# Query, key and value projections as products of float32r parts, and an earlier split of the second head's maxima

## Time and profile before

| what | value |
|---|---|
| median of 3 runs | 775.11 us (773.37 to 775.14) |
| profiled execution | 772.37 us, of which the span of instructions is 770.6 us |
| busy in the span | PE 707.3 us (92%), DVE 586.9 (76%), ACT 487.0 (63%), POOL 132.5 (17%) |
| granted TensorE clock | 0.995 of full, over the span |

### The profile page before, as it was taken

One profiled execution on the slowest core, in us unless ns is written; L12 is line 12 of the kernel. 1 busy time (PEld: TensorE's weight loads), 2 busy tenths in 40 slices (PEclk: granted clock), 3 DMA queues, 4 the chain that ended last, 5 costly groups with the idle time before them and its releaser, 6 DMA issues.

```text
span 770.6 us, 14200 instructions
## 1 busy us (share of the span) xinstructions
PE 707.3 (92%) x3976; PEld 373.9 (49%) x3977; DVE 586.9 (76%) x800; ACT 487.0 (63%) x886; POOL 132.5 (17%) x282
## 2 busy tenths in 40 slices
PE   5999999799889888998998888799999999998997
PEld 2456544522222222221222212388888888887886
DVE  5375588799999889899999984378777777756764
ACT  2472600388888888888888878656656665646321
POOL 1000000756531111011111111000000000005730
PEclk9999999999999999999999999999999999999999
DMA  9729100177411111011110172041111111122420
GB/s 316 246 68 328 44 1 0 47 234 235 130 48 32 32 32 32 17 32 32 32 32 24 38 262 90 15 151 44 51 54 49 46 54 54 54 90 81 143 92 28
DMA packets 49951, 65.35 MB, mean 85 GB/s; under 512 B 8168, under 2 KB 42880, under 8 KB 49920
## 3 DMA queue, kind: packets, MB, share of 16 engines
q1 hardware_dynamic: 38848, 40.85, 16.7%
q10 hardware_dynamic: 8000, 15.73, 6.2%
q0 software_dynamic: 3072, 8.39, 3.5%
HBM read 40.15 MB, written 24.38 MB: 84 GB/s over the span
## 4 chain that ended last, share of the span: by engine, by line
PE 76%; ACT 10%; issue 5%; DVE 5%; POOL 1%; DMA 1%; ACTq 1%; SPq 0%; DVEq 0%; POOLq 0%
PE ps L1386 14%; PE ps L1357 14%; ACT att L729 9%; PE ps L1410 9%; PE ps L1456 9%; PE ps L1238 7%; PE ps L1488 6%; DVE smax L993 3%; PE ps L1230 3%; PE ps L1503 3%; PE ps L1447 2%; PE ps L1198 2%; PE ps L1263 2%; PE ps L1346 1%; POOL acc L557 1%
## 5 line engine op out<-in xcount | busy, mean ns | idle before, releaser
L993 DVE TENSOR_REDUCE smax<-ps 128x2 f32<-128x1024 f32 x256 | 302.5, 1221 | 36.3 <-PE ps L1263 33.2
L729 ACT ACTIVATE att<-ps 128x512 f32<-128x512 f32 x512 | 267.7, 602 | 54.6 <-PE ps L1410 51.8
L1410 PE MATMUL ps<-att 51*128 51x512 bf16 x512 | 165.8, 384 | 32.8 <-ACT att L729 19.3
L1263 PE MATMUL ps<-att 48*128 48x512 bf16 x512 | 163.5, 386 | 1.4 <-DVE smax L993 1.4
L1357 PE MATMUL ps<-att,v_head 128*32 128x512 f32 x1024 | 137.1, 608 | 1.7 <-ACT o_sb L688 0.6
L1410 PEld LDWEIGHTS ps<-att 51*128 51x128 bf16 x512 | 39.7, 93 | 201.6 <-ACT att L729 95.8
L1386 PE MATMUL ps<-att_r 128*128 128x512 f32 x456 | 117.5, 406 | 3.1 <-DVE att_r L1054 1.6
L1050 DVE TENSOR_TENSOR att_r<-big,att_r 128x1024 fp32r<-128x1024 f32 x76 | 89.8, 1222 | 23.9 <-ACT att_r L709 23.8
L1386 PEld LDWEIGHTS ps<-att_r 128*128 128x128 f32 x456 | 85.5, 188 | 21.4 <-DVE att_r L1054 2.1
L709 ACT ACTIVATE att_r<-big 128x1024 fp32r x74 | 74.3, 1051 | 19.0 <-issue 19.0
L1456 PE MATMUL ps<-big,xn 128*128 x312 | 73.7, 380 | 0.0
(11 more groups left out here) (164 smaller groups left out, 691.1 us busy)
## 6 DMA issues: line engine op xcount, KB each, us to landing
big<-w ACTq DMA_DIRECT2D x8, 1024.0 KB
q_stacks<-big SPq DMA_DIRECT2D x12, 512.0 KB
att<-q_stacks SPq DMA_DIRECT2D x64, 96.0 KB, 2.1
slot_x<-zeros SPq DMA_DIRECT2D x1, 4992.0 KB, 17.2
e_x<-slot_x SPq DMA_DIRECT2D x39, 128.0 KB, 2.0
slot_y<-xn SPq DMA_DIRECT2D x39, 128.0 KB, 1.7
big<-w ACTq DMA_DIRECT2D x8, 512.0 KB
att<-k_stacks SPq DMA_DIRECT2D x64, 48.0 KB, 2.0
```

Source lines behind the costliest of these rows:

```text
L729: act.activation(probs[:, t % 2, g, :], ps[:, RING[turn_of(u) % 3], :], ACT.Exp, scale=SCALE)\
L993: dve.reduce_max(smax[:, s % 2, :].rearrange("p (half v) -> p half v", half=2)[:, :, v], ps[:, bank:bank + 2, :], X_AXIS).then_inc(max_don ...
L1263: return pe.matmul(ps[:, bank + half, :], q_st[s][rows, g, P * st:P * (st + 1)], k_st[s][rows, :], start=True, stop=True)
L1410: pe.matmul(ps[:, RING[turn % 3], :], k_st[s][rows, P * t:P * (t + 1)], q_st[s][rows, g, :], start=True, stop=True).then_inc(scores_ready, 1)
```

## The change

The weights of the three projections are rounded to float32r on ScalarE (`pw_hi`), and VectorE subtracts for the rest (`pw_lo`). For each quarter ScalarE rounds the two transposed banks (`round_xT`, into `p_hi`) in front of the two copies to `xnT`, and VectorE subtracts for the rest (`rest_of_xT`, into `p_lo`), with two buffers that alternate by quarter. A unit becomes three products of two matmuls each: hi weights by hi tokens, lo weights by hi tokens, hi weights by lo tokens. ScalarE's square roots stand one quarter earlier in its list. On GpSimd `split_max(1, 1)` stands in front of the memory sums. TensorE's own wait for the four loads moves from the first unit to the router matmuls; ScalarE waits for them before it rounds the weights.

```diff
@@ gpsimd
             split_max(0, 0)
             stage_v(0, 0, 0, 0)
+            split_max(1, 1)
             pool.wait_ge(s_add, 2 * 4)
@@ def steps
-                    if not (first and s == 0):
+                    if not (first and s < 2):
                         split_max(i, s)
+                    if not (first and s == 0):
                         stage_v(i, b, h0 + s, s)
@@ scalar
+            def round_xT(n):
+                act.wait_ge(xT_in_psum, n + 1)
+                if n >= 4:
+                    act.wait_ge(qk_in_psum, UNITS[n // 2 - 2][1])
+                act.activation(p_hi[n // 2 % 2][:, n % 2, :], ps[:, n % 4, :], ACT.Copy).then_inc(p_hi_ready, 1)
+            sqrt_var(0)
+            act.wait_ge(proj_loaded, 64)
+            act.activation(pw_hi[:, :, 0:2 * P], wq_sb, ACT.Copy)
+            act.activation(pw_hi[:, :, 2 * P:3 * P], wkv_sb, ACT.Copy).then_inc(pw_hi_ready, 1)
             for n in range(4):
-                sqrt_var(n)
+                if n < 3:
+                    sqrt_var(n + 1)
+                round_xT(2 * n)
+                round_xT(2 * n + 1)
                 copy_xT(2 * n)
                 copy_xT(2 * n + 1)
@@ vector
+            def rest_of_xT(n):
+                for m in (2 * n, 2 * n + 1):
+                    dve.wait_ge(xT_copied, m + 1)
+                    dve.tensor_tensor(p_lo[n % 2][:, m % 2, :], xnT[:, m % 2, 512 * n:512 * (n + 1)],
+                                      p_hi[n % 2][:, m % 2, :], ALU.subtract).then_inc(p_lo_ready, 1)
@@ at the end of quarter n's list, behind the writes of xn
+                if n == 0:
+                    dve.wait_ge(pw_hi_ready, 1)
+                    dve.tensor_tensor(pw_lo[:, :, 0:2 * P], wq_sb, pw_hi[:, :, 0:2 * P], ALU.subtract)
+                    dve.tensor_tensor(pw_lo[:, :, 2 * P:3 * P], wkv_sb, pw_hi[:, :, 2 * P:3 * P], ALU.subtract)\
+                       .then_inc(pw_lo_ready, 1)
+                else:
+                    rest_of_xT(n - 1)
+            rest_of_xT(3)
@@ tensor, project_qk
-                pe.wait_ge(xT_copied, 2 * n + 2)
                 wait(pe, qk_copied, u - 3)
-                for k in range(KD):
-                    tokens = xnT[:, k, 512 * n:512 * (n + 1)]
...
+                column = 2 * P if part == 0 else P * (part - 1)
+                for count, (ws, w_sem, xs, x_sem) in enumerate((
+                        (pw_hi, pw_hi_ready, p_hi, p_hi_ready), (pw_lo, pw_lo_ready, p_hi, p_hi_ready),
+                        (pw_hi, pw_hi_ready, p_lo, p_lo_ready))):
+                    pe.wait_ge(w_sem, 1)
+                    pe.wait_ge(x_sem, 2 * n + 2)
+                    for k in range(KD):
+                        last = pe.matmul(ps[:, 4 + u % 4, :], ws[:, k, column:column + P], xs[n % 2][:, k, :],
+                                         start=count == 0 and k == 0, stop=count == 2 and k == KD - 1)
                 last.then_inc(qk_in_psum, 1)
             for n in range(4):
                 transpose_xn(n)
-                if n == 0:
-                    pe.wait_ge(proj_loaded, 64)
                 for u in range(*UNITS[n]):
                     project_qk(u)
+            pe.wait_ge(proj_loaded, 64)
+            pe.wait_ge(xT_copied, 8)
```

More of the change, by code:

```diff
@@ L156, in build @@
         wkv_sb = big[:, 22016:22272].rearrange("p (k n) -> p k n", k=KD)
+        p_hi, p_lo = [[split[:, 4096 + 2048 * a + 1024 * n:5120 + 2048 * a + 1024 * n]
+                       .rearrange("p (k n) -> p k n", k=KD) for a in range(2)] for n in range(2)]
+        pw_hi, pw_lo = [split[:, 8192 + 768 * n:8960 + 768 * n].rearrange("p (k n) -> p k n", k=KD) for n in range(2)]
         mtmp = big[:, 4096:6144].rearrange("p (a d) -> p a d", a=8)
@@ L222, in build @@
         xT_copied = sem("xT_copied")
+        pw_hi_ready = sem("pw_hi_ready")
+        pw_lo_ready = sem("pw_lo_ready")
+        p_hi_ready = sem("p_hi_ready")
+        p_lo_ready = sem("p_lo_ready")
         lT_in_psum = sem("lT_in_psum")
@@ L569, in steps @@
                     i = blk * 4 + s
+                    if not (first and s < 2):
+                        split_max(i, s)
                     if not (first and s == 0):
-                        split_max(i, s)
                         stage_v(i, b, h0 + s, s)
```

## The result

The changed kernel takes 776.68 us (median of 10 runs, 776.06 to 777.46) against 773.96 for the kernel before in the same runs: a ratio of 1.0034, 95% interval 1.0024 to 1.0044, so 2.7 us more (1.9 to 3.4). The forecast was 776.3 us. The profiled execution has a span of 775.0 us against 770.6. I read it as before: the chain first, then the timelines of the two stretches.

What follows compares the result with a forecast made beforehand. TensorE was taken to bound the kernel, owning 76% of the chain. First stage plus 4.0, GpSimd's move minus 2.8, gives 1.2 more on a median of 775.11: 776.3 us, range 773.2 to 779.6.

Steps and rivals of the forecast that it cites:

- the first stage: Projections, up to the router matmuls: claimed plus 4.0 us, bounds 3.2 and 5.1, ending at 41.2 instead of 37.17.
- one of my signs of being wrong: First stage: the prediction would be wrong if the stage ended more than 5 us late.
- The move: GpSimd's second split in front of the memory sums: claimed minus 2.8 us, bounds 1.7 and 3.1, at no cost.
- The late start: Start of the projections: TensorE's first product at 16.75, 5.2 us later than the first unit did.
- my upper bound for the quarter: First quarter's products: if all eight remaining ran at half rate, they would end at 23.1 instead of 22.0.
- the rival that I gave 0.18: First stage: the clock stays at 1.2 GHz to the end of unit 2, some 2.7 us more, 779.0; chance 0.18.
- the wait on copies: Last quarter: unit 9 waits for ScalarE's copy of unit 5, leaving TensorE 1.35 us idle.
- VectorE's rests: Projection quarters: TensorE stands 0.7 to 0.8 us in each, waiting for VectorE's subtractions that give the tokens' rests.
- TensorE's price: Projection units: six float32r matmuls take 1.375 us instead of 1.72, saving 0.345 each, 4.1 us over twelve units.
- The shift goes on to the end: From 41 to 138 us: nothing absorbs the first stage's delay, so plus 4.0 us reaches the kernel's end.
- The rival that it is absorbed: Between 41 and 138 us: an independent wait absorbs the first stage's shift, leaving only minus 2.8, 772.3; chance 0.12.
- The rival that it brings nothing: Behind the memory sums: something else is as late as the split, so no gain, 779.1 us; chance 0.08.

Runs made afterwards that it cites:

- e1: The kernel before with only GpSimd's second split moved in front of the memory sums: 769.76 us, ratio 0.9956 to the kernel before.
- e3: Changed kernel with the second quarter's statistics ahead of the rests of the weights and ScalarE's second root before its load wait: 772.81 us, ratio 0.9985.
- e4: Changed kernel with 40 extra float32 matmuls, results thrown away, on TensorE while it waits for the first product: 775.98 us, ratio 1.0025.
- e5: Changed kernel with ScalarE's copies of finished units in front of the next quarter's rounding: 776.14 us, ratio 1.0034.
- e6: Changed kernel with finished units copied first, token rests taken straight from PSUM, and copies to xnT waiting for them: 774.40 us, ratio 1.0005.
- e7: Changed kernel with finished units copied first, rests from PSUM, and second-quarter statistics and root moved ahead: 770.12 us, ratio 0.9950 to the kernel before.
- e9: The kernel before (float32 projections) with the split moved, five filler matmuls and a separate semaphore for the router load: 768.94 us, ratio 0.9930.
- e8: Changed kernel with copies, rests and statistics reordered, plus five filler matmuls, separate router semaphore, tokens rounded before weights, token rests earlier: 766.64 us, ratio 0.9920.
- e2: Changed kernel with GpSimd's second split back behind the memory sums, so the projections' part alone: 780.18 us, ratio 1.0085 to the kernel before.
- e10: The kernel before with ten bf16 matmuls, results thrown away, filling TensorE's wait for the second split: 770.84 us, ratio 0.9962.

## Why the prediction was right, and where it was not

**The direction and the total.** The forecast of 776.3 lies 0.4 under the measured 776.68, and that is luck: two errors of opposite sign. It was built on a median of three runs, 775.11, where ten gave 773.96, so 1.15 too high; and the change was put at 1.2 us more where 2.7 were measured, so 1.5 too low. The direction came as the sum had it. Slower by 0.34% lies just past the 0.3% that I took for the least that can be told, and to that side I gave 0.35, to no change 0.53; the measured interval is 0.1% to either side, so my 0.3% was too wide.

By the terms the forecast was worse than by the total. Counted from the landing the first stage costs 6.9 to 7.0 us (32.50 against 25.60 in the kernel before and 25.50 in e1), not 4.0, and outside my bounds of 3.2 and 5.1; one of my signs of being wrong, a stage that ends more than 5 us late, came true (router matmuls at 44.87 against 37.10). The move gives 2.9, and the sum is 4.0 to 4.1 more, not 1.2.

The two profiles differ by 4.4 us and the medians by 2.7, because of which executions were profiled: that of the kernel before took 772.37 us, 1.6 under its median, that of the changed kernel 776.79, at its median. The granted clock goes with this. In the three rounds of experiments the kernel before ran 62 times; the 14 runs at 0.995, the clock of the profiled one, have a median of 772.77, and the 35 at 0.993 one of 774.51. None of the changed kernel's ten runs lies under 0.995. So most runs of the kernel before spend more time at the lower clock than its profile shows; where, they do not show.

**The late start was right.** VectorE's wait for the rounded weights held back the second quarter's statistics, the root behind it held back the rounding, and the first product stood 5.3 us behind the landing (5.2 forecast). e3 moved the statistics and the start came to 2.1 us behind it.

**The first stage was mis-sized in two terms.** The forecast had the quarters end 10.5, 16.2, 21.9 and 29.7 us after the landing; they ended 11.5, 18.2, 24.6 and 32.5 after it. First, the clock: I let the full rate come within the first quarter's eight products; they and the transposes behind them ran at the lower rate to the end. That is my upper bound for the quarter, and part of the rival that I gave 0.18. e4, the same kernel at the full rate, prices it at 2.4 us; 0.8 of them were in my sum, 1.6 were not. Second, the wait on copies: I saw it for unit 9 and missed the same one at unit 6 (34.14 in the timeline above), which makes the third quarter 6.4 us and not 5.7. I also took VectorE's rests as a gap of 0.7 to 0.8 in every quarter; TensorE stood 0.60 and 0.28 us for them in the first two and not at all later, where the copies were later still. e5 shows they are the next thing in line, so that removing the wait on copies alone wins 0.5 us. Removing both (e6) wins 3.2, and with the start (e7) 7.7 from the landing, which is the whole loss and 0.7 more.

**TensorE's price was right in the difference.** From a row's start to the next row's, a product takes 0.237 us, not 0.229 (twenty-four in 5.69 us in e6), so a unit 1.42. The float32 unit takes 1.76 by the same count and not 1.72 (e9: 21.93 us from 15.03 to 36.96 less three times 0.87 for transposes, eleven units). The difference is the forecast 0.34 us, 4.1 over twelve units; e8 against e9 shows 3.5 of them. One slip in the prediction has no consequence: the row of 3.78 us in the earlier trace rows has four records, two float32 matmuls, so it is one unit and not two.

**The shift goes on to the end: right.** From the router matmuls to the first scores all twelve profiles take 109.02 to 109.12 us, and in e2 the median rose by 6.6 us (5.6 to 7.6) for a stage that is 6.9 longer. The rival that it is absorbed falls.

**The move: right in mechanism and size**, 2.9 us against 2.8, and it costs GpSimd nothing. The rival that it brings nothing falls with e1. One reason was too simple: I took the clock to stay up when the gap of 2.41 us goes. It stayed up in five of nine profiles of kernels with the move (11.90 us to the third transpose) and fell in four (13.1 to 13.4), without any long gap; in the changed kernel's profile it stayed up. The row on which I rested this, a gap of 1.54 us that did no harm in the earlier trace rows, does not hold from one execution to the next. The same row in the changed kernel (timeline of TensorE, 460 to 530 us):

```profile
500.18 4.58 PE L1425 MATMUL ps<-att_r 128*128 128x512 f32 x12 [1.54 <-issue]
```

Behind the same gap of 1.54 us these twelve products take 4.45 to 4.59 us in eight of the twelve profiles and 2.99 to 3.01 in the other four (before, e6, e7, e10).

## What to carry to other kernels

Splitting an operand for faster products adds a chain of round, subtract and copy on other engines, and its place in their lists matters more than the products: look at what an in-order engine must finish before the new instruction, and what stands queued behind it. When a gap is named by one releaser, work out what is next in line before it is priced; here two waits of nearly the same length hid each other. Give a wait to the instruction that needs it: TensorE's first matmul and then ScalarE's rounding waited for a router weight that is used 25 us later.

## What the runs showed of the hardware that was not expected

The granted clock falls to 0.50 (1.2 GHz) at the same place of the code in some executions and not in others. In the stretch of short bf16 matmuls behind the memory sums it fell in both profiles with a gap of 2.4 us in front (before, e2), in four of nine without that gap (in e3 with no idleness above 0.39 us in the 10 us ahead), and not in the one where the gap was filled (e10). At the first products of the experts it fell in eight profiles of twelve. Runs of one kernel differ too: over the span, the changed kernel's ten show 0.995 to 0.999. The Trainium skill (TensorE: Matmul & The Clock Gate, Part 1) says of the start of a kernel that the number of matmuls at the lower rate differs from run to run of one kernel. The traces agree: the first float32 unit, up to which their code is the same, took 3.78 us (before), 3.68 (e1) and 3.40 (e10). What decides a fall further on, no run here shows.

In the first stage the column of the granted clock shows 1.00 while the rows run at half rate (3.75 us against 2.07 for eight products), so there the durations have to be read, not the column.
